# A graph-attention and expert layer on one core: x's statistics taken apart over two steps, the first and third norm's roots made together

## The reference, cut to what matters

```
xn   = layernorm(x)                                  # norm 1
q, k, v = xn @ Wq.T + bq, xn @ Wk.T + bk, xn @ Wv.T + bv      # 4 heads of 32
s    = clip(q k.T / sqrt(32), -10, 10); s = where(adj == 0, -10, s)
attn = softmax over each chunk of 128 keys (8 chunks), ctx = attn v
o    = (ctx summed over chunks) @ Wo.T + bo + xn
x2   = x + layernorm(o) * gamma + beta               # norm 2
y    = layernorm(x2)                                 # norm 3
top two of 8 experts by y @ Wg + bg; out = x2 + sum of both gelu(y W1 + b1) W2 + b2
```

## Time and profile before

| | us |
|---|---|
| median of 3 runs (lowest to highest) | 784.2 (783.95 to 785.22) |
| the profiled execution: its time | 785.9 |
| its span in the trace | 784.1 |
| busy: PE, DVE, ACT, POOL | 699.3, 630.9, 490.3, 588.5 |

### The profile page before, as it was taken

The page is one execution under the profiler, slowest core; times in us unless marked ns, Lnnn a source line. Parts: engine busy times, 40 slices in busy tenths (PEclk is TensorE's granted clock), DMA queues, the critical chain, the costliest instruction groups (busy, mean ns, idle before and its releaser), DMA issues.

```text
span 784.1 us, 17077 instructions
## 1 busy us (share of the span) xinstructions
PE 699.3 (89%) x5416; PEld 364.8 (47%) x5416; DVE 630.9 (80%) x1479; ACT 490.3 (63%) x874; POOL 588.5 (75%) x711
## 2 busy tenths in 40 slices
PE   4898899999999999999999999895978879999994
PEld 2222223333333333333333333231668769999994
DVE  4799989999999999999999989999895545545552
ACT  4665676766767667676666775553646426666763
POOL 7778495887978879788797987969577345666664
PEclk9999999999999999999999999999989879999998
DMA  7620000111010010101100001040313223333330
GB/s 269 198 74 28 15 15 14 35 35 41 16 42 28 29 54 15 41 22 35 55 15 28 14 29 41 15 137 28 90 61 94 73 79 96 85 87 96 95 92 1
DMA packets 47960, 45.44 MB, mean 58 GB/s; under 512 B 6981, under 2 KB 42576, under 8 KB 47872
## 3 DMA queue, kind: packets, MB, share of 16 engines
q1 hardware_dynamic: 41888, 31.60, 14.4%
q0 software_dynamic: 5984, 12.74, 4.5%
HBM read 27.73 MB, written 18.34 MB: 59 GB/s over the span
## 4 chain that ended last, share of the span: by engine, by line
DVE 34%; PE 24%; issue 22%; POOL 8%; ACT 7%; DMA 2%; DVEq 1%; another core or an unknown queue 1%; POOLq 0%; ACTq 0%
DVE e L879 15%; PE scores_ps L417 7%; DVE ctx_part L887 6%; PE scores_ps L574 5%; POOL out L1331 4%; DVE ln_stats L851 4%; ACT e L709 3%; ACT x_rows L714 3%; PE z_ps L600 2%; PE ctx_ps L600 2%; DMA near<-in_x 2%; PE ctx_ps L429 2%; DVE ln_mv L855 2%; PE z_ps L436 2%; DVE best_at L935 1%
## 5 line engine op out<-in xcount | busy, mean ns | idle before, releaser
L709 ACT ACTIVATE e<-e 128x2048 f32<-128x2048 f32 x128 | 244.8, 1912 | 180.6 <-DVE e L879 180.5
L879 DVE SCALAR_TENSOR_TENSOR e<-scores_ps,bound_mem 128x2048 f32<-128x2048 f32 x128 | 292.2, 2283 | 29.3 <-PE scores_ps L417 29.2
L1304 POOL TENSOR_TENSOR ctx_part<-ctx_part,z_inv 128x1024 f32<-128x1024 f32 x60 | 116.7, 1945 | 57.0 <-DVE z_inv L895 57.0
L774 ACT ACTIVATE e<-scores_ps,bound_mem 128x128 f32<-128x128 f32 x364 | 104.2, 372 | 77.7 <-PE scores_ps L574 63.8
L1331 POOL DMA_INDIRECT out<-e,near x91 | 91.3, 1004 | 70.1 <-DVE e L1075 27.6
L436 PE MATMUL z_ps<-e,one_column 128*32 128x512 f32 x1024 | 133.7, 594 | 0.0
L1316 POOL TENSOR_TENSOR ctx_sum<-ctx_sum,ctx_part 128x512 f32<-128x512 f32 x90 | 115.6, 1285 | 7.0 <-POOL ctx_sum L1316 0.4
L574 PE MATMUL scores_ps<-e,bound_mem 128*128 128x128 f32 x728 | 101.1, 284 | 6.7 <-DVE bound_mem L1057 5.9
L574 PEld LDWEIGHTS scores_ps<-e,bound_mem 128*128 128x128 f32 x728 | 92.3, 199 | 9.3 <-issue 6.4
L887 DVE STREAM_TRANSPOSE ctx_part<-ctx_ps 128x512 f32<-128x512 f32 x128 | 90.3, 705 | 0.0
L1278 POOL DMA_INDIRECT sorted_rows<-x_rows,slot x64 | 64.1, 1001 | 23.8 <-issue 21.9
(11 more groups left out here) (167 smaller groups left out, 1010.4 us busy)
## 6 DMA issues: line engine op xcount, KB each, us to landing
near<-sorted_rows SPq DMA_DIRECT2D x91, 130.0 KB
near<-in_x SPq DMA_DIRECT2D x16, 256.0 KB, 2.9
bound_mem<-in_adjT SPq DMA_DIRECT2D x4, 1024.0 KB, 9.3
x_post<-in_x SPq DMA_DIRECT2D x16, 256.0 KB, 2.7
sorted_rows<-pad_row SPq DMA_DIRECT2D x1, 3640.0 KB, 15.1
out<-e,near POOLq DMA_INDIRECT x91
sorted_rows<-x_rows,slot POOLq DMA_INDIRECT x64
bound_mem<-in_w SPq DMA_DIRECT2D x1, 1024.0 KB
```

The lines of the kernel that those rows point to most:

```text
L709: nc.scalar.activation(every, every, ACT.Exp, scale=SCORE_SCALE).then_inc(exp_done, 1)
L774: nc.scalar.activation(e_flat[:, h_at:h_at + P], scores_ps[:, i % 2, k * P:(k + 1) * P], ACT.Gelu, bias=part_flat[:, bias_at:bias_at + 1]) ...
L879: dve.scalar_tensor_tensor(out=e[:, s % E_RING], in0=scores_ps[:], scalar=-CLIP, in1=to, op0=ALU.max, op1=ALU.min).then_inc(clipped, 1)
L1304: nc.gpsimd.tensor_tensor(pair, pair, z_inv[:, v % 2, j:j + 2].to_broadcast([P, 2, SQUARES, DH]), ALU.mult).then_inc(ctx_scaled, 1)
```

## The change

Two edits.

1. **`statistics` is cut in two.** `begin_statistics` is the four `bn_stats`, `end_statistics` the rest. Norms 2 and 3 still call both at once. For norm 1 in the main loop the first part stays at `j = 3` and the second goes to `j = 4`, behind that step's `clip` and `turn`. It concerns the blocks `u = 0` to `12`, where there is a block `u + 3`.
2. **`root_both`.** The small tiles of norms 1 and 3 (`mv`, `minus`, `var`, `rstd`, `shift`) become two halves of tiles twice as wide. In the blocks `u = 2` to `12` (11 of them) one `minus` and one `rstd` over 128 x 8 numbers serve both norms, at the place of norm 3's root. Two `shift` of 128 x 4 follow, norm 3's first. The separate root of norm 1 behind `add_context(u - 1, 7)` is gone there. In the other blocks `root` is as before.

```diff
-        minus_half = sb("minus_half", [P, TILES, 1])
-        minus_one = sb("minus_one", [P, TILES, 1])
+        minus_half = sb("minus_half", [P, 2 * TILES, 1])
+        minus_one = sb("minus_one", [P, 2 * TILES, 1])
...
-            def statistics(l, v, src):
+            def begin_statistics(l, v, src):
                 need(dve, l["s_out"], v)
                 for t in range(TILES):
                     ins = dve.bn_stats(l["stats"][:, t, :], src[:, t, :])
                 ins.then_inc(l["s_stats"], 1)
+
+            def end_statistics(l, v):
                 dve.wait_ge(l["s_stats"], v + 1)
                 for t in range(TILES):
                     ins = dve.bn_aggr(l["mv"][:, t, 0:2], l["stats"][:, t, :])
...
                     if j == 3 and is_block(u + 3):
-                        statistics_x(u + 3)
+                        dve.wait_ge(x_loaded[(u + 3) % 2], 16 * ((u + 3) // 2 + 1))
+                        begin_statistics(ln["1"], u + 3, x_in[:, (u + 3) % 2])
+                    if j == 4 and is_block(u + 3):
+                        end_statistics(ln["1"], u + 3)
...
+            def root_both(v1, v3):
+                for l, v in ((ln["1"], v1), (ln["3"], v3)):
+                    pool.wait_ge(l["s_var"], v + 1)
+                    need(pool, l["s_out"], v)
+                roots["both"] += 1
+                nc.gpsimd.tensor_tensor(both["minus"][:], both["mv"][:, :, 0:1], minus_one[:], ALU.mult)\
+                    .then_inc(both_minus, 1)
+                nc.gpsimd.tensor_tensor(both["rstd"][:], both["var"][:], minus_half[:], ALU.pow).then_inc(both_rstd, 1)
+                pool.wait_ge(both_minus, roots["both"])
+                pool.wait_ge(both_rstd, roots["both"])
+                for l in (ln["3"], ln["1"]):
+                    nc.gpsimd.tensor_tensor(l["shift"][:], l["minus"][:], l["rstd"][:], ALU.mult)\
+                        .then_inc(l["s_shift"], 1)
...
-                if is_block(u - 2):
+                if is_block(u - 2) and is_block(u + 3):
+                    root_both(u + 3, u - 2)
+                elif is_block(u - 2):
                     root(ln["3"], u - 2)
                 if is_block(u - 1):
                     add_context(u - 1, 6)
                     add_context(u - 1, 7)
-                if is_block(u + 3):
+                if is_block(u + 3) and not is_block(u - 2):
                     root(ln["1"], u + 3)
```

More of the change, by code:

```diff
@@ L1 @@
+import collections
 from contextlib import ExitStack
@@ L201, in graph_transformer_layer @@
         ln = {}
+        both = {name: sb(f"ln13_{name}", [P, 2 * TILES, size])
+                for name, size in (("mv", 3), ("minus", 1), ("var", 1), ("rstd", 1), ("shift", 1))}
         for n in ("1", "2", "3"):
-            ln[n] = dict(stats=sb(f"ln{n}_stats", [P, TILES, 6]), mv=sb(f"ln{n}_mv", [P, TILES, 3]),
-                         minus=sb(f"ln{n}_minus", [P, TILES, 1]), var=sb(f"ln{n}_var", [P, TILES, 1]),
-                         rstd=sb(f"ln{n}_rstd", [P, TILES, 1]), shift=sb(f"ln{n}_shift", [P, TILES, 1]),
+            if n == "2":
+                of = {name: sb(f"ln2_{name}", [P, TILES, size])
+                      for name, size in (("mv", 3), ("minus", 1), ("var", 1), ("rstd", 1), ("shift", 1))}
+            else:
+                at = int(n) // 3 * TILES
+                of = {name: both[name][:, at:at + TILES, :] for name in both}
+            ln[n] = dict(stats=sb(f"ln{n}_stats", [P, TILES, 6]), **of,
                          s_stats=sem(f"ln{n}_stats_ready"), s_mv=sem(f"ln{n}_mv_ready"),
@@ L208, in graph_transformer_layer @@
                          s_rstd=sem(f"ln{n}_rstd_ready"), s_shift=sem(f"ln{n}_shift_ready"),
-                         s_out=sem(f"ln{n}_out_ready"))
+                         s_out=sem(f"ln{n}_out_ready"), name=n)
         scores_ps = bank("scores_ps", [P, HEADS, BLOCK])
@@ L325, in graph_transformer_layer @@
         out_stored = sems("out_stored", XT_RING)
+        both_minus, both_rstd = sem("both_minus_ready"), sem("both_rstd_ready")
         HALF0_D = CHUNKS // 2
@@ L860, in statistics @@
                 dve.tensor_reduce(l["var"][:, :, 0], l["mv"][:, :, 1:3], AXIS.X, ALU.add).then_inc(l["s_var"], 1)
+            def statistics(l, v, src):
+                begin_statistics(l, v, src)
+                end_statistics(l, v)
             def prepare_bound(half, c):
@@ L1260, in prepare_bound @@
                     .then_inc(bound_p, 1)
+            roots = collections.Counter()
+            def root_both(v1, v3):
[11 more added lines that the diff above has]
+                        .then_inc(l["s_shift"], 1)
             def root(l, v):
@@ L1265, in root @@
                 pool.wait_ge(one_ready, 1)
-                nc.gpsimd.tensor_tensor(l["minus"][:], l["mv"][:, :, 0:1], minus_one[:], ALU.mult)\
+                roots[l["name"]] += 1
+                nc.gpsimd.tensor_tensor(l["minus"][:], l["mv"][:, :, 0:1], minus_one[:, 0:TILES], ALU.mult)\
                     .then_inc(l["s_minus"], 1)
-                nc.gpsimd.tensor_tensor(l["rstd"][:], l["var"][:], minus_half[:], ALU.pow).then_inc(l["s_rstd"], 1)
-                pool.wait_ge(l["s_minus"], v + 1)
-                pool.wait_ge(l["s_rstd"], v + 1)
+                nc.gpsimd.tensor_tensor(l["rstd"][:], l["var"][:], minus_half[:, 0:TILES], ALU.pow)\
+                    .then_inc(l["s_rstd"], 1)
+                pool.wait_ge(l["s_minus"], roots[l["name"]])
+                pool.wait_ge(l["s_rstd"], roots[l["name"]])
                 nc.gpsimd.tensor_tensor(l["shift"][:], l["minus"][:], l["rstd"][:], ALU.mult).then_inc(l["s_shift"], 1)
```

## The result

The changed kernel takes 793.2 us (median of 4 runs, 792.55 to 794.01) against 784.15 for the kernel before: 1.0117 times as long, 95% interval 1.0102 to 1.0131. It is 9 us slower. The prediction was 791.7, slower, with a range up to 793.2; the measured time stands at its upper edge. The profiled execution took 793.1 with a span of 791.1, 7.0 more than the span before.

What follows compares the result with a forecast made beforehand. No engine is full; each step is a ring of DVE's clip and PE's scores, at least 3.62 us. The joint root costs 11 x 0.68 = 7.5, the split's 1.49 is swallowed: 784.2 + 7.5 = 791.7, range 782.4 to 793.2.

Steps and rivals of the forecast that it cites:

- The split's worth: Steps 3 and 4: moving statistics wins 0.19 in odd and 0.09 in even blocks, 1.49 us, until PE's values job is late.
- It is swallowed by the joint root: The split's gain of 1.49 us is lost, because both lines in step 7 hang on POOL, whose start step 1 sets.
- Both edits' sign, and where it hurts: Slower, chance 0.74; in step 7 ACT waits for norm 3's shift (0.68 a block), DVE for the last ctx_sum (0.64).
- d = 0.82: Growth of rstd from four to eight numbers a partition, 0.205 us for each number; the forecast's own case, chance 0.60.
- The second rival: Joint rstd on POOL: cost part fixed, part per number, growth 0.4, so 2.9 us more and 787.1; chance 0.10.
- the argument against a fixed price: On rstd: a fixed price has no visible source, since minus, 0.20 us in all, pays the same start and end.
- The line of step 7: ACT's normalise_x2, PE's transposes and next scores move by rstd's growth plus 0.05 for waits less 0.19 slack: 0.68 a block.
- So what is removed there is worth nothing by itself.: Norm 1's minus (0.20) and rstd (1.02) behind the last ctx_sum: POOL waits 2.32 for DVE anyway before the next scaling.
- The sum: Whole kernel: 11 blocks x 0.68 = 7.5 us more, the split's 1.49 swallowed, 784.2 + 7.5 = 791.7.
- The rival by the page's rule: Four more numbers add about 0.01 us to rstd; sum as with a per-instruction cost (783.0, chance 0.25); no own chance.

Runs made afterwards that it cites:

- fill_ahead2: Changed kernel plus the old root's three instructions on scratch numbers ahead of the scatter in blocks 2 to 12; 790.6 us, ratio 1.0089 to the kernel before.
- pow_widths: Kernel before plus scratch powers and products of 1 to 64 numbers on POOL behind its last store; 842.7 us, no comparison.
- fill_last: Changed kernel plus three scratch instructions between third and fourth scatter instruction, blocks 2 to 12; 777.4 us, ratio 1.0065 to the kernel before (772.7).
- fill_middle: Changed kernel plus three scratch instructions between second and third scatter instruction; 779.8 us, ratio 1.0114 to the kernel before.
- split_again: Second run of the changed kernel with both roots apart at their old places and widths; 771.7 us against 772.3 for the kernel before, ratio 0.9999.
- split_only: Changed kernel with both roots apart at their old places and widths; 782.6 us against 784.0 for the kernel before, ratio 0.9988.

## Why the prediction was right or wrong

- **The split's worth, 0.19 and 0.09 a block, bounded by PE's values job.** Right; measured 0.18 and 0.09 alone. Block 13, which lacked the work that was to be moved, was a good stand-in.
- **It is swallowed by the joint root.** Right: the kernels with and without the split have blocks of the same length.
- **Both edits' sign, and where it hurts.** Right: ACT waits for the `shift`, DVE for the last `ctx_sum`, and they end together (354.06 is 1.28 behind PE's scores and directly behind `turn_sum`).
- **d = 0.82.** The step that failed is "So 0.20 covers starting, finishing and moving four numbers, and the other 0.82 must be the power itself." The power has a fixed part of its own: 0.42 in all where the product has 0.19. The second rival, part fixed and part per number, thus had the form right and the size wrong (d = 0.4), and the argument against a fixed price, that `minus` pays the same start and end, doesn't hold. d = 1.65 - 1.02 = 0.63. The line of step 7 then gives 0.63 + 0.05 - 0.19 = 0.49 a block; with the delay of step 0 taken out (fill_ahead2) a block takes 33.56, which is 0.44 more than 33.12. The line of waits was right and d was taken 0.19 too large: 11 x 0.44 = 4.8 instead of 7.5 (in that trace blocks 2 to 13 take 400.9 against 396.3, which is 4.6).
- **"So what is removed there is worth nothing by itself."** This is the other step that failed, and no rival foresaw it: the removal was put at nothing because only the next block's first scaling was looked at, and not the scatter that stands in between. It was worth less than nothing. With norm 1's root gone from behind the last `ctx_sum`, the scatter comes 1.5 us earlier against DVE's step and delays two of its instructions: on average 0.38 a block in blocks 5 to 13, 3.4 us. It is shown by putting the distance back, by moving the fourth scatter alone, and by moving the third and fourth together.
- **The sum.** 4.8 + 3.4 = 8.2, which is what blocks 2 to 13 lost (8.2); the medians differ by 9.0 and the profiled spans by 7.0. That the total came near was luck: an overestimate of 2.7 and an omission of 3.4 nearly cancel. Each alone would have given some 789 or 795.
- **The rival by the page's rule.** The Trainium skill ("GPSIMD Engine Reference", section 3.1) was weighed with 2.6 cycles an element for a two-input `tensor_tensor`. The product agrees (0.002 us a number from 4 to 64); the power's 0.158 is some 75 times that, so that rival fell.

## What to carry to other kernels

Merging two small instructions saves only the part that is paid once, and the merged one must wait for both inputs and makes both readers wait: measure the part paid once with a row of widths before counting on it, and look whether the copy that is removed stood on the path at all. An instruction in idle time may still be what holds the next ones at a harmless distance; when it is removed, look at what runs beside the work that moves up, above all at DMAs that POOL issues. Where a block lacks a piece of work (the first, the last ones), the kernel's own trace holds the experiment already: block 13 gave the right number for the first edit, and steps 0 of 5.08 and 5.32 in blocks 14 and 15 would have warned of the delay.

## What the runs showed of the hardware

- **A power on POOL is 0.42 us and 0.158 us a number** of each partition, straight to within 0.05 up to 64 numbers; a product is 0.19 and 0.002 (pow_widths).
- **An indirect scatter from POOL can hold up the start of a DVE instruction.** `gates`, ready at 2.84, started at 2.93 where the third scatter instruction ran from 2.01 to 2.97, and at 3.04 (block 6) where it ran from 2.15 to 3.11: just before its end. It takes a narrow coincidence: where the third started at 1.82 to 1.88 (blocks 14 and 15) or at 2.18 to 2.21 (block 4), `gates` started at 2.84. The clip, ready near 4.97, started at 5.23 where the fourth had started at 3.28. That one's own instruction was over at 4.24, but its rows were being moved: in the 0.6 us from 4.80 on (window 358.86 to 359.46) the DMA queue that POOL fills has the following. That the moving rows, and not the instruction before them, hold the clip up is read from these times alone.

```profile
q0 software_dynamic: 48, 0.13, 61.0%
```

  In block 4 of the changed kernel, where the fourth started at 3.47 and its rows moved from 5.0 on, the clip started at 4.85, ahead of them and without delay:

```profile
152.84 0.96 POOL L1315 DMA_INDIRECT sorted_rows<-x_rows,slot  x1 [0.30 <-issue]
153.48 0.26 DVE L943 TENSOR_TENSOR gates<-job_ps,bg_row 128x140 f32<-128x140 f32 x1
154.11 0.96 POOL L1315 DMA_INDIRECT sorted_rows<-x_rows,slot  x1 [0.30 <-issue]
...
155.49 2.28 DVE L895 SCALAR_TENSOR_TENSOR e<-scores_ps,bound_mem 128x2048 f32<-128x2048 f32 x1
```

  Which part of the chip is shared is open. The Trainium skill ("SBUF — State Buffer", "Who interferes with whom") says that a DVE instruction with at most one input in SBUF and outside the two-port modes doesn't contend with GpSimd. Both delayed instructions have one input in PSUM and one in SBUF, so by that rule they should not have been held up; the rows say that their start was.
- **The delay isn't always there.** In the traces taken where the kernel before took 784 or 785, every clip of blocks 14 and 15 was late (step 0 at 4.92 to 5.32). In the three with an early scatter taken where it took 772 or 773 (fill_last, fill_middle, split_again), none was. In block 14 of split_again the fourth scatter starts at 3.11 and its rows move from 4.6 to 5.1, as in the changed kernel, where it starts at 3.12; the clip starts at 4.84 in the one and at 5.07 in the other. The faster traces gain their time elsewhere: the same kernel takes 267.7 from the first clip of block 15 to the end in split_only and 257.0 in split_again, while the steps of the middle blocks agree to 0.01. A given chip isn't shown to be the cause: the record has the same chip number, 10, for 784.0 (split_only) and, later, 772.7 (fill_last). What differs wasn't found.
